# Two fp32r parts, heads side by side, one block for projection and attention, and a table look-up on POOL

## The reference, cut to what matters

```python
q = compute_rope((x @ W_Q.T).reshape(B, S, 16, 16)); k, v: 8 heads of 16
scores = einsum('bsdkg,btdk->bkgst', q, k) / sqrt(256)
ctx = einsum('bkgst,btdk->bkgsd', softmax(scores, -1), v);  s = ctx @ W_O.T
gate = x @ lut[gate_idx].T; up = x @ lut[up_idx].T          # 688 x 256 indices each
ffn = (silu(gate) * up) @ lut[down_idx].T
```

## Time and profile before

| | us |
|---|---|
| median of 3 runs | 1137.59 (1137.35 to 1137.98) |
| span of the profiled execution, first to last instruction | 1137.0 |
| what the median has above that span | 0.6 |
| PE busy in it | 1029.0 |
| DVE, ACT, POOL busy | 730.6, 489.1, 378.5 |

### The profile page before, as it was taken

How to read it: one execution, slowest core, us unless ns; L and a number is a source line. 1 busy time by engine, 2 the same in 40 slices (tenths; PEclk the granted TensorE clock), 3 DMA queues, 4 the chain that set the end, 5 groups by cost and what they waited for, 6 DMA issues and landing times. The chain is left out here.

```text
span 1137.0 us, 18228 instructions
## 1 busy us (share of the span) xinstructions
PE 1029.0 (91%) x7112; PEld 625.2 (55%) x7112; DVE 730.6 (64%) x993; ACT 489.1 (43%) x864; POOL 378.5 (33%) x304
## 2 busy tenths in 40 slices
PE   4869999999999999998999999846899999999997
PEld 3722333333333333322687878745756788888886
DVE  6889777778777877770376554499923574434433
ACT  1412666666556555656542244130621343332322
POOL 3231444346434543456011000296600042323232
PEclk9866999999999999999999999865599999999999
DMA  4580111111111111100200000230000111211211
GB/s 164 179 276 19 31 33 33 34 28 33 32 33 32 33 33 33 37 12 12 69 1 1 2 1 1 77 126 3 2 3 1 47 59 35 74 47 57 65 56 47
DMA packets 43606, 52.87 MB, mean 46 GB/s; under 512 B 14216, under 2 KB 30472, under 8 KB 43256
## 3 DMA queue, kind: packets, MB, share of 16 engines
q1 hardware_dynamic: 43104, 50.99, 14.4%
q10 hardware_dynamic: 416, 0.72, 0.2%
HBM read 37.53 MB, written 12.06 MB: 44 GB/s over the span
## 5 line engine op out<-in xcount | busy, mean ns | idle before, releaser
L626 DVE TENSOR_REDUCE row_max<-psum 128x1 f32<-128x1024 f32 x256 | 302.6, 1218 | 87.5 <-PE psum L679 87.4
L611 ACT ACTIVATE probs_t<-psum 128x512 f32<-128x512 f32 x512 | 267.1, 603 | 199.9 <-PE psum L693 199.9
L703 PE MATMUL psum<-probs_t,VS 128*32 128x512 f32 x1024 | 206.9, 604 | 17.5 <-ACT o_sb L494 17.5
L581 POOL TENSOR_TENSOR lut_sum<-lut_sum,lut_tmp 128x1072 f32<-128x1072 f32 x60 | 149.4, 2490 | 200.1 <-DVE lut_tmp L644 199.4
L679 PE MATMUL psum<-KS,QS 96*128 96x512 bf16 x512 | 164.6, 405 | 13.0 <-DVE row_max L626 8.9
L693 PE MATMUL psum<-QS,KS 99*128 99x512 bf16 x512 | 153.7, 381 | 3.2 <-ACT probs_t L611 3.2
L1858 POOL TENSOR_TENSOR m_h_f<-m_h_f,comb_b 128x512 f32<-128x512 f32 x44 | 71.5, 1625 | 234.0 <-DVE m_h_f L1936 234.0
L679 PEld LDWEIGHTS psum<-KS,QS 96*128 96x128 bf16 x512 | 39.0, 98 | 158.7 <-DVE row_max L626 114.6
L1936 DVE TENSOR_TENSOR m_h_f<-psum,m_silu 128x512 f32<-128x512 f32 x56 | 38.7, 691 | 124.9 <-ACT m_silu L1893 124.9
L693 PEld LDWEIGHTS psum<-QS,KS 99*128 99x128 bf16 x512 | 48.9, 97 | 99.9 <-ACT probs_t L611 49.9
L1893 ACT ACTIVATE m_silu<-psum 128x512 f32<-128x512 f32 x56 | 33.4, 597 | 154.7 <-PE psum L392 154.7
(11 more groups left out here) (228 smaller groups left out, 1729.4 us busy)
## 6 DMA issues: line engine op xcount, KB each, us to landing
QS<-q_rows SPq DMA_DIRECT2D x32, 192.0 KB
m_raw<-experts_w SPq DMA_DIRECT2D x2, 2688.0 KB, 13.0
comb_b<-comb_rows SPq DMA_DIRECT2D x16, 256.0 KB, 3.3
q_rows<-part SPq DMA_DIRECT2D x8, 384.0 KB, 3.1
KS<-k_rows SPq DMA_DIRECT2D x16, 192.0 KB
x_tok<-x SPq DMA_DIRECT2D x4, 512.0 KB, 7.9
q_rows<-part SPq DMA_DIRECT2D x8, 256.0 KB, 4.0
ctxT<-o_sb SPq DMA_DIRECT2D x64, 32.0 KB, 2.0
```

The source lines that it names most:

```text
L581: nc.gpsimd.tensor_tensor(wsum[:, cols], wsum[:, cols], wtmp[:, slot % 3, :], ALU.add).then_inc(lut_add, 1)
L611: nc.scalar.activation(pt[:, k % NPT, :], ring(k)[:], ACT.Exp, scale=float(E) ** -0.5).then_inc(p_ready, 1)
L626: nc.vector.tensor_reduce(mx[:, n % 2, i:i + 1], m.psum[:, 2 * (k % 2):2 * (k % 2) + 2, :], AX_XY, ALU.max).then_inc(max_done, 1)
L703: nc.tensor.matmul(OB[32 * j:32 * (j + 1), :], m.VS[:, bb * NTT + t, kv, :], pt[:, k % NPT, :], start=(t == 0), stop=(t == NTT - 1)).then_ ...
```

## The change

q and k are split into two fp32r parts instead of three bf16 ones: three products of 16 rows are 48 rows, and the two parts of the maximum make 50. The two heads of a group stand on partitions 0 and 64, four buffers deep, and the keys are loaded for both. Projection and attention are one block; scaling goes from DVE to ACT, the low part is made on POOL, and V of the last two token blocks is projected among the first maxima. The look-up goes to POOL as a whole, from indices that ACT makes fp32. `weigh` comes in two halves of 256 queries. In time mix both heads' V matmuls go ahead of both heads' state matmuls. The steps of the projection run in these orders:

```diff
+Q_SLOTS = (HI, HI, LO)
+K_SLOTS = (LO, HI, HI)
+NROW = len(Q_SLOTS) * HD
+NAUG = NROW + NPART
+HEAD_ROWS = 64
+NQK = 4
...
+    m.QS = [at(f"QS{i}", [P, S], F32R, m.qk_at + i * S * 4) for i in range(NQK)]
+    m.KS = [at(f"KS{i}", [P, S], F32R, m.qk_at + (NQK + i) * S * 4) for i in range(NQK)]
...
+        for g in range(G):
+            rows = slice(g * HEAD_ROWS, g * HEAD_ROWS + NROW)
+            sp.dma_start(m.KS[q][rows, :].bitcast(F32), m.k_rows[:, kv * HD:(kv + 1) * HD, seq]
...
+    def low_parts(pool, tb):
+        for u in range(3):
+            pool.wait_ge(part_hi, 3 * tb + u + 1)
+            nc.gpsimd.tensor_tensor(part[:, tb % 2, u, 1, :], rot[:, u, :], part[:, tb % 2, u, 0, :],
+                                    ALU.subtract).then_inc(part_lo, 1)
...
-            nc.vector.tensor_tensor(res[:, u, :], rot[:, u, :], part[:, tb % 2, u, 0, :],
-                                    ALU.subtract).then_inc(resid, 1)
...
-    AHEAD = NST // 2
+    AHEAD = 10
+    FLOAT_AT = (0, 2, 6, 10)
+    PAIRED = (2, 3, 0, 1)
...
                 if n + 1 < NG:
                     place_max(n + 1)
+                if n >= 1:
+                    spread(sp, n - 1)
+        def look_up(pool, k):
...
+            nc.gpsimd.tensor_scalar(wsum[:, c % 2, :] if v == 0 else wtmp[:, slot % 2, :],
+                                    idxf[:, c * PIECE:(c + 1) * PIECE], float(v), lut[:, v:v + 1],
+                                    ALU.is_equal, ALU.mult).then_inc(lut_prod, 1)
...
+            nc.gpsimd.tensor_tensor(wsum[:, c % 2, :], wsum[:, c % 2, :], wtmp[:, slot % 2, :],
+                                    ALU.add).then_inc(lut_add, 1)
...
+                if n + 1 < NG:
+                    max_parts(pool, n + 1)
+                for k in range(4 * n, 4 * n + 4):
+                    look_up(pool, k)
...
+                    if i == 20 and n in FLOAT_AT:
+                        nc.scalar.activation(idxf[:, cols], idx[:, cols], ACT.Copy).then_inc(idx_float, 1)
...
             for k in range(NST + AHEAD):
-                maxima_ahead(k)
+                maximum(k, 0)
+                maximum(k, 1)
+                if k == NST // 4:
+                    m.project_v(pe, 2)
+                if k == NST // 2:
+                    m.project_v(pe, 3)
             for n in range(NG):
                 for t in range(NTT):
+                    s = n * NTT + t
+                    k = (n + 1) * NST + AHEAD + G * t
+                    for h in range(2):
+                        maximum(k, h)
+                        scores(n, t, h)
+                    if s >= 1:
+                        weigh(*divmod(s - 1, NTT), 0)
+                    for h in range(2):
+                        scores(n, t, 2 + h)
+                        maximum(k + 1, h)
+                    if s >= 1:
+                        weigh(*divmod(s - 1, NTT), 1)
...
                 for c in range(NC):
                     for h in range(NH):
+                        mm = nc.tensor.matmul(out(c, h), m.V[:, bb * NC + c, ct * P + h * LD:ct * P + (h + 1) * LD],
+                                              A[g][:, h * NC + c, :], start=True, stop=(c == 0))
+                    for h in range(NH if c else 0):
                         ch = slice(h * LD, (h + 1) * LD)
+                        mm = nc.tensor.matmul(out(c, h), ST[g % 2][ch, c, :], group(m.R, g)[ch, c * CH:(c + 1) * CH],
+                                              start=False, stop=True)
```

More of the change, by code:

```diff
@@ L683, in scores, with rows, maximum @@
[L683 to L687 removed]
+            m.project_tensor(pe)
+            pe.wait_ge(m.ones_ready, NQK)
+            def rows(g, n):
+                return slice(g * HEAD_ROWS, g * HEAD_ROWS + n)
+            def maximum(k, h):
+                if k >= NG * NST:
+                    return
+                n, i = divmod(k, NST)
+                if i == 0 and h == 0:
+                    pe.wait_ge(qk_in[n % NQK], 16 * m.LOADS * (n // NQK + 1))
+                if k >= 2 and h == 0:
+                    pe.wait_ge(max_done, k - 1)
+                if k == 1 and h == 0:
+                    pe.wait_ge(m.v_out, 2 * TPB)
+                st, g = divmod(i, G)
+                mm = nc.tensor.matmul(MX[k % 2][h][:], QS[n % NQK][rows(g, NROW), st * P:(st + 1) * P],
+                                      KS[n % NQK][rows(g, NROW), h * BLK:(h + 1) * BLK], start=True, stop=True)
+                if h == 1:
+                    mm.then_inc(max_ps, 1)
@@ L692, in scores, with weigh @@
                     pe.wait_ge(p_ready, k - 2)
-                nc.tensor.matmul(ring(k)[:], KS[n % 3][:, t * P:(t + 1) * P], QS[n % 3][:, j * BLK:(j + 1) * BLK],
+                nc.tensor.matmul(ring(k)[:], KS[n % NQK][rows(g, NAUG), t * P:(t + 1) * P],
+                                 QS[n % NQK][rows(g, NAUG), half * BLK:(half + 1) * BLK],
                                  start=True, stop=True).then_inc(s_ps, 1)
-            def weigh(n, t):
+            def weigh(n, t, part):
                 bb, kv = divmod(n, KV)
-                for j in range(NJ):
-                    k = (n * NTT + t) * NJ + j
-                    pe.wait_ge(p_ready, k + 1)
-                    if t == 0 and j == 0 and n >= 1:
-                        pe.wait_ge(o_done, n)
-                    nc.tensor.matmul(OB[32 * j:32 * (j + 1), :], m.VS[:, bb * NTT + t, kv, :], pt[:, k % NPT, :],
-                                     start=(t == 0), stop=(t == NTT - 1)).then_inc(pv_done, 1)
@@ L706, in maxima_ahead @@
-            def maxima_ahead(k):
-                if k < NG * NST:
-                    maxima(k // NST, k % NST)
-            for k in range(NST + AHEAD):
-                maxima_ahead(k)
+                cols = slice(part * BLK // 2, (part + 1) * BLK // 2)
+                for i in range(NJ):
+                    k = (n * NTT + t) * NJ + i
+                    j = PAIRED[i]
+                    if part == 0:
+                        pe.wait_ge(p_ready, k + 1)
+                        if t == 0 and i == 0 and n >= 1:
+                            pe.wait_ge(o_done, n)
+                    mm = nc.tensor.matmul(OB[32 * j:32 * (j + 1), cols], m.VS[:, bb * NTT + t, kv, :],
+                                          pt[:, k % NPT, cols], start=(t == 0 and part == 0),
+                                          stop=(t == NTT - 1 and part == 1))
+                    if part == 1:
+                        mm.then_inc(pv_done, 1)
@@ L729, in ffn_stage @@
+                    if s >= 1:
+                        weigh(*divmod(s - 1, NTT), 1)
+            for part in range(2):
+                weigh(NG - 1, NTT - 1, part)
 def ffn_stage(nc, m, a):
```

538 lines of the change are left out of this document (262 added, 276 removed).

## The result

The changed kernel takes 1132.53 us (median of 7 runs, 1127.18 to 1137.09) beside 1137.98 for the kernel before (7 runs, 1137.35 to 1141.61): ratio 0.994, 95% interval 0.9917 to 0.9964. It is faster by 0.6%, where 980 us was forecast. The profiled execution took 1127.18 us, and its span is 1125.3, 1.9 less; the 0.6 that the prediction put above the span compared the median of the runs with the span of one other execution. Runs that were disturbed, or fell into a slower state, are left out of the ratios.

The account below looks back on a forecast made before the run. The attention loop was taken as bound by a ring of PE and ACT, no engine saturated. From a span of 1137.0: loop -127.5, ahead of it -11, time mix -19, giving 979.5; forecast 980 us, range 950 to 1050.

Parts of the forecast that it names:

- The step that failed: Attention loop: a look-up pass of compare and multiply over 128x1072 fp32 on POOL takes 1.72 us, bounds 0.95 to 5.0.
- first rival: Attention loop: with a look-up of 2.5 us POOL sets the pace; loop 363 us, time 1021; chance 0.15.
- third rival: Attention loop: POOL's look-up costs a us, its chain 206.6 + 64 a; 1184 us at a = 5.0; chance 0.03.
- Loop: Attention loop: 322 us against 449.5, -127.5, with DVE's row maxima the latest at 2.35 us a step.
- POOL's tail: End of the attention block: POOL's last look-ups and sums end 7 us after PE.
- Ahead of the loop: Before the first score: DVE loses scaling and residues, row maxima start at 55 instead of 71.5; -11 us, bounds 0 and -20.
- Time mix: Time mix's output: both heads' matmul pairs side by side, two times 0.36 us a chunk instead of four; -19 us.
- From the loop's end to time mix's output: Stretch between attention loop and time mix's output: no change was forecast, 0 us.
- Pairs: Attention loop: a maximum and a score on different partitions stream at once, 0.235 us a pair.
- The halves: Attention loop: the weighted sum in two halves, with scores ahead of the second, brings the ring to 2.05 us.
- the ring: Attention loop: exponentials, last column group of the weighted sum, two maxima and a score follow each other, 3.47 us a step.
- The half clock: Attention loop: PE's granted clock at 0.50, a step 4.0 us, the loop 516, the time 1173; chance 0.02.

Follow-up runs that it names:

- the run with the pass of 1.71 us: Changed kernel with POOL's look-up products cut to 424 of the 1072 columns, the rest of the look-up left out: 1014.5 us, ratio 0.891.
- the first experiment: Changed kernel with the look-up products moved back from POOL to DVE, POOL keeping the sums: median 1053.7 us in four runs (1029.7 to 1056.3).

## Why the prediction was wrong

**The step that failed** is "I take 1.72, halfway between fill and sum, since it reads one tensor", the price of the look-up on POOL. It measured 3.91. All that hung on it followed the prediction's own first rival, POOL's pace: its group formula, 4 x (3.91 + 2.57) + 1.2 = 27.1 us, is what the loop shows (451 / 16 = 28.2), and the formula of the third rival, 206.6 + 64 a, gives 457 us for POOL's chain where 451 was measured. The mechanism had been named and its bounds (0.95 to 5.0) held the value; the choice within them was by counting inputs, and the inputs don't set the price. The one row of the same instruction, the TENSOR_SCALAR of 32 elements, pointed the right way: its 143 ns over a copy are 4.5 ns an element, and 3.39 were measured. It was set aside as "far". By the first rival's own line, 64 us of loop for each us of the pass, 3.91 makes 1111 us; the later start (+13) and the way to time mix (+4) lead from there to the 1127 of the profiled execution. The forecast's range (950 to 1050) cut off the upper part of that rival, and with it the result, which lies above even the 1120 that the rival was given.

The other terms, against the run with the pass of 1.71 us, whose span is 1011.2 where the forecast was 979.5:

- **Loop**, forecast 322, measured 335.4. The step measured 2.46 for 2.35 to 2.45, but by other terms, so that its hit is in part **luck**: a pair takes 0.33 us and not 0.235, half a sum 0.57 and not 0.63, PE's sum is 2.46 and not 2.2, and PE is last, not DVE (24.53 and 23.84 of 25 us busy). A group takes 20.25 us and not 19.6 (14 groups from 129.53 to 413.08), which is 9 of the 13 us; the last one takes 18.8 and not 17, and the first 12 us, at half clock, cost more than the 4 us that were added. POOL's tail, 6.5 us after PE, came as forecast (7).
- **Ahead of the loop**, forecast -11, measured +2.3 in the changed kernel: **wrong**. The maxima start at 59 instead of 55, and the two V projections cost 5.23 us each and not 3 in all. The clock was to be seen in the earlier trace rows: 0.50 in this stretch before, too. With them ahead of the maxima the first score comes at 95.2, still 6.4 after the forecast 88.8.
- **Time mix**, forecast -19, measured -20: **right**, by the reason given.
- **From the loop's end to time mix's output**, forecast 0, measured +4.2: the stage begins half-clocked after PE's wait for POOL.
- **Pairs**, taken as overlapping: **right** (0.0 us apart), though at 0.33 us and not at the price of one stream. **The halves** as what "buys the ring": **mostly wrong**; with whole sums the step is down from 3.47 to 2.61 already, and the halves bring it to 2.46.
- **The half clock**, held at 0.02 as a rival of its own for the whole loop: it came in stretches, behind waits of PE. The 4.0 us that the prediction gave such a step measured 4.32.

The start (+14 against the forecast), the loop (+13) and the way to time mix (+5 in that run) make the 32 us between the forecast's span and that run's; the pass makes the other 118 of the median.

What stays open is when the clock falls and why a half-clocked stretch ends where it does. PE has gaps in the kernel before, too (13.84 of 15 us busy in 120 to 135), and the clock stays at 1.00 there, so a gap alone does not decide it. After a gap the half clock lasted some 20 us in the first experiment (241 to 261) and some 60 at its end (422 to 481), with PE busy 20.00 of 20 and 59.00 of 59 us.

## What to carry to other kernels

A pass moved to another engine is priced by a row of the same operation pair on that engine, however small its tile, and not by the number of its inputs; where the bounds lie on both sides of the point at which that engine becomes the bound, the range has to reach over it. A fast DVE pass between SBUF tiles belongs where POOL is idle, since a collision costs the rest of POOL's operation and holds what stands behind the pass. And after each stall on PE's path the granted clock is to be read for the next tens of microseconds, for the stall may cost more there than it lasted.

## What the runs showed of the hardware

- POOL's 128x1072 fp32 pass: 1.08 to 1.16 us for a copy or a pair of add and multiply, 2.92 to 2.94 for any single operation that was tried, 3.83 to 3.91 for pairs with a comparison, a maximum or a subtraction. One operation costs 2.7 times as much as two of the right ones. The Trainium skill (GPSIMD Engine Reference, 3.1) has 1.03 cycles an element for up to two operations: at 1.2 GHz that is an estimate of 0.92 us, and the copy and the pairs of add and multiply come near it (1.08); the comparison's 3.39 ns an element, some four cycles, do not, and the measurement decides.
- A DVE product from SBUF to SBUF that starts under a POOL operation takes up to 2.92 us instead of 0.68 to 0.77.
- Through the loop, the same matmuls of 48 and 50 rows ran at a granted clock of 1.00 in pairs on different partitions, and at 0.50 one after another, PE busy throughout (719.86 of 720 us). At the end of the loop, scores one after another ran at 1.00 in one run (24.71 of 25 us busy) and at 0.50 in another (25.00 of 25).
- Two matmuls of 512 columns on different partitions start within 0.01 us of each other; the pair takes 0.33 us at a granted clock of 1.00.
